# Matmuls that fill PE's waits before the dispatch, a joint dispatch of four tiles, and four small moves of other work

## The reference

```python
x = x + _L0_xattn_ref(_layernorm(x), ctx_1024, ctx_1024, ...)   # 16 heads, softmax over 1024 keys
x = x + _L0_attn_ref(_layernorm(x), ...)                        # S4 convolution over the 8 batches, then silu
x = x + _L0_ffn_ref(_layernorm(x), ...)                         # 16 experts, each token weighs its best 4
x = x + _L1_xattn_ref(_layernorm(x), ctx_1024, ctx_1024, mask, gamma, beta)
x = x + _L1_attn_ref(_layernorm(x), ...)                        # Mamba: conv, step size, recurrence h = At * h + Xt
x = x + _L1_ffn_ref(_layernorm(x), ...)                         # 8 experts top 2, and a shared one
```

## Time and profile before

| | us |
|---|---|
| median of 3 runs | 731.85 (731.85 to 731.97) |
| the profiled execution | 729.76 |
| its span, first to last instruction | 728.0 |
| granted TensorE clock, mean | 0.987 |

### The profile page before, as it was taken

The page is one execution under the profiler, slowest core; times in us unless marked ns, Lnnn a source line. Parts: engine busy times, 40 slices in busy tenths (PEclk is TensorE's granted clock), DMA queues, the critical chain, the costliest instruction groups (busy, mean ns, idle before and its releaser), DMA issues.

```text
span 728.0 us, 15573 instructions
## 1 busy us (share of the span) xinstructions
PE 683.5 (94%) x5722; PEld 558.3 (77%) x5722; DVE 539.4 (74%) x1205; ACT 412.5 (57%) x790; POOL 432.3 (59%) x455
## 2 busy tenths in 40 slices
PE   6799999999999978699999999999999899999997
PEld 3577777777787767599999999997457466666786
DVE  5788787877787886037777777763657899998676
ACT  3565756656655542266666666652336886665442
POOL 4658634646456226567788778745414698898130
PEclk9999999999999999799999999999999999999999
DMA  8301101101009392599989898995784610001000
GB/s 343 118 2 59 59 1 58 50 8 58 0 0 354 118 386 92 213 370 381 396 335 336 327 350 340 335 362 183 285 343 153 234 59 1 0 1 45 1 0 30
DMA packets 20477, 123.51 MB, mean 170 GB/s; under 512 B 2288, under 2 KB 6784, under 8 KB 13120
## 3 DMA queue, kind: packets, MB, share of 16 engines
q1 hardware_dynamic: 17488, 114.72, 41.4%
q0 software_dynamic: 2928, 8.00, 3.0%
HBM read 111.90 MB, written 10.81 MB: 169 GB/s over the span
## 4 chain that ended last, share of the span: by engine, by line
PE 77%; DVE 10%; ACT 5%; POOL 4%; issue 3%; DMA 1%; another core or an unknown queue 0%; DVEq 0%; SPq 0%; ACTq 0%; POOLq 0%; PEldq 0%
PE banks L2233 66%; PE banks L2301 8%; DVE shown L2094 2%; POOL inject L1016 2%; DVE banks L2101 1%; DVE negmax_raw L1618 1%; PE banks L2532 1%; ACT banks L1385 1%; PE banks L2848 1%; ACT probs L1097 1%; DMA table<-in_table 1%; DVE shown L2111 1%; ACT turned_back L1396 1%; PE banks L2688 0%
## 5 line engine op out<-in xcount | busy, mean ns | idle before, releaser
L2233 PE MATMUL banks<-xT,raw 128*128 128x128 f32 x992 | 151.6, 276 | 0.6 <-DVE xT L1882 0.6
L2233 PEld LDWEIGHTS banks<-xT,raw 128*128 128x128 f32 x992 | 135.5, 192 | 3.5 <-issue 1.1
L947 POOL TENSOR_TENSOR w_lo<-raw,w_hi 128x1024 fp32r<-128x1024 f32 x50 | 118.0, 2383 | 1.8 <-ACT w_hi L1217 1.0
L1248 ACT ACTIVATE banks<-banks,later 128x128 f32<-128x128 f32 x200 | 67.9, 339 | 56.3 <-PE banks L2233 54.9
L1888 DVE CAST mid_hi<-banks 128x128 fp32r<-128x128 f32 x200 | 57.8, 289 | 33.6 <-ACT banks L1248 31.8
L1127 ACT ACTIVATE probsT<-banks 128x512 f32<-128x512 f32 x68 | 40.1, 597 | 73.4 <-PE banks L2301 73.2
L1016 POOL TENSOR_TENSOR inject<-BCbc,drive 128x1024 f32<-128x1024 f32 x31 | 72.7, 2362 | 13.0 <-DVE shown L2094 7.7
L1097 ACT ACTIVATE probs<-banks,negmax 128x1024 f32<-128x1024 f32 x64 | 71.2, 1112 | 12.2 <-DVE negmax L1620 10.3
L1618 DVE TENSOR_REDUCE negmax_raw<-banks 128x1 f32<-128x1024 f32 x64 | 77.5, 1211 | 0.6 <-PE banks L2233 0.6
L2233 PE MATMUL banks<-w_hi,mid_hi 128*128 128x256 f32 x200 | 72.5, 362 | 0.0
L2301 PE MATMUL banks<-table,probs 128*128 128x128 f32 x512 | 69.6, 279 | 0.7 <-DVE probsT L1591 0.7
(11 more groups left out here) (358 smaller groups left out, 1763.7 us busy)
## 6 DMA issues: line engine op xcount, KB each, us to landing
raw<-in_w SPq DMA_DIRECT2D x31, 2048.0 KB, 8.9
ctx_raw<-in_ctxT SPq DMA_DIRECT2D x8, 1024.0 KB, 4.8
ctxT<-in_ctxT SPq DMA_DIRECT2D x4, 2048.0 KB, 9.3
ctxN<-in_ctxN SPq DMA_DIRECT2D x4, 2048.0 KB, 13.5
x_slots<-zero SPq DMA_DIRECT2D x1, 3968.0 KB, 12.5
y_slots<-y_tile POOLq DMA_DIRECT2D x29, 128.0 KB, 7.0
wf<-in_w SPq DMA_DIRECT2D x9, 384.0 KB, 5.3
BCbc<-bc_rows SPq DMA_DIRECT2D x6, 512.0 KB, 6.8
```

The lines of the kernel that those rows point to most:

```text
L947: nc.gpsimd.tensor_tensor(w2_lo[i % WB][:, cols], raw[i % WB][:, EW // 2:][:, cols], w2_hi[i % 2][:, cols].bitcast(F32), ALU.subtract).the ...
L1248: nc.scalar.activation(to, held, ACT.Gelu, bias=b1[:, bass.ds(at + u, 1)]).then_inc(gelu_done, 1)
L2233: return nc.tensor.matmul(o, lhsT, rhs, start=start, stop=stop)
```

## The change

1. `run_on` issues a float32 matmul of the identity with 128 or 256 columns of `later` into a bank that is free. Nine of them stand between and behind the routing's pieces (three of 128 columns), and three in `count_rows` (one of 128) (its bank is now called COUNT_BANK, still 3). No result uses them.
2. `largest` gets four more columns, filled once with the lowest value; `match_replace` reads columns 0 to 3 and 8 to 11. The four `memset`s are gone.
3. HOT is 5: `hot_rest` has four tiles, `dispatch_rest` multiplies 512 columns and stands at n = 4 (REST_AT). `x_rows` is read from tile 5 on; its place in memory stays (ROWS_FROM = 4). The spreads are turned at (3, 0) and (3, 4), four units later.
4. The mask terms are made in quarters behind the stores of tiles 6 to 13.
5. `step_end` becomes `step_size` and `step_drive`; for the step of chunks 2 and 3 the first stands one unit earlier. The skip term of chunks 0 to 2 stands behind `turn_states` of g = 7.
6. In the first batch ACT makes part 0 of the second batch's `ctx_hi` ahead of the second exponential.
7. The two late splits are made in halves, behind units 26, 27 and 29, 30.

```diff
-HOT = 4
+HOT, REST_AT = 5, 4
+ROWS_FROM = 4
-LAST = 2
+LAST, MASK_FROM = 2, 6
-SPREAD_AT = tuple(UNITS * i + u for i, u in ((2, 4), (3, 0)))
+SPREAD_AT = tuple(UNITS * i + u for i, u in ((3, 0), (3, 4)))
-SKIP_AT = (6, 6, 6, 4)
+LAST_SKIP = 4
...
-                if i < 2:
-                    mask_term(i)
+                if MASK_FROM <= i < MASK_FROM + 8:
+                    mask_term(*divmod(i - MASK_FROM, 4))
...
-                    if n - 1 in SPLIT1_AT:
-                        split_low1(SPLIT1_AT[n - 1])
-                    if g == GROUPS // 2 and m + 1 < CC:
-                        step_end(m + 1)
+                    for half in range(2):
+                        if n - 1 - half in SPLIT1_AT:
+                            split_low1_half(SPLIT1_AT[n - 1 - half], half)
+                    if m + 1 < CC:
+                        if g == GROUPS // 2 - (1 if m else 0):
+                            step_size(m + 1)
+                        if g == GROUPS // 2:
+                            step_drive(m + 1)
...
-                    if d == 0 and later_one:
-                        context_high(b + 1, 1 - par, range(1, DC))
+                    if d == 0:
+                        context_high(b + 1, 1 - par, range(1, DC) if later_one else range(1))
...
-                    if d == 0 and not later_one:
-                        context_high(b + 1, 1 - par)
+                        context_high(b + 1, 1 - par, range(1, DC))
...
-                    order.step(nc.vector.max(largest[:, t, :], logits[:, t, :]))
-                    order.step(nc.vector.memset(largest[:, t, TOP0:], LOWEST))
-                    order.mark(nc.vector.match_replace(left[:, t, :], largest[:, t, :], ranked[:, t, :], TAKEN))
+                    order.step(nc.vector.max(largest[:, t, 0:8], logits[:, t, :]))
+                    first_four = largest[:, t, :].rearrange("p (a b) -> p a b", b=TOP0)[:, 0::2, :]
+                    order.mark(nc.vector.match_replace(left[:, t, :], first_four, ranked[:, t, :], TAKEN))
...
+                run_on(SQUARE_BANK, 1, P)
                 pe.wait_ge(sel_ready, sel_before + 2)
...
+                run_on(SQUARE_BANK, 2)
+
+            def run_on(bank, times=1, columns=D):
+
+                for _ in range(times):
+                    mm(pb(bank)[:, 0:columns], ident, later[:, 0:columns], True, True)
...
             turn_tokens(3, 0, ROUTE_BANKS)
+            run_on(LOGIT_BANKS[2], 1, P)
             turn_tokens(3, 1, ROUTE_BANKS)
...
+            run_on(LOGIT_BANKS[2])
+            route(0)
+            run_on(LOGIT_BANKS[2])
+            turn_tokens(3, 2, ROUTE_BANKS)
+            run_on(LOGIT_BANKS[2], 1, P)
+            route(1)
+            turn_tokens(3, 3, ROUTE_BANKS)
+            run_on(COUNT_BANK, 1, P)
+            route(2)
+            run_on(COUNT_BANK)
+            route(3)
+            run_on(COUNT_BANK, 3)
...
-                if n == 1:
+                if n == REST_AT:
                     dispatch_rest()
...
-                if g == SKIP_AT[m]:
-                    pe.wait_ge(skip_made, 2 * GS + m + 1)
-                    mm(pb(Y_BANK), skip_diag[:, m * P:(m + 1) * P], aT[:, m, :], False, False)
+                if m == CC - 1 and g == LAST_SKIP:
+                    add_skip(m)
...
+                    if m < CC - 1 and g == GROUPS - 2:
+                        add_skip(m)
```

More of the change, by code:

```diff
@@ L331, in build @@
                 mask += [sb("phase", f"mask{q}", [P, KEYS], I32) for q in range(2, TC)]
-                assert mask_at >= aliased + (X_PIECES[2] - HOT) * D * 4 and place["phase"] <= aliased + (TILES - WB + 2 - HOT) * D * 4
+                assert mask_at >= aliased + (X_PIECES[2] - ROWS_FROM) * D * 4 and place["phase"] <= aliased + (TILES - WB + 2 - ROWS_FROM) * D * 4
             ctxN2.append(sb("phase" if p else "stage", f"ctxN2{p}", [P, 2, KC, D]))
@@ L1043, in split_low1, with split_low1_half @@
                 nc.gpsimd.tensor_tensor(f_lo[n][:], wf[n][:], f_hi[n][:].bitcast(F32), ALU.subtract).then_inc(f_lo_ready, 1)
+            def split_low1_half(n, half):
+                if half == 0:
+                    pool.wait_ge(f_hi_ready, n + 1)
+                cols = slice(half * FW // 2, (half + 1) * FW // 2)
+                done = nc.gpsimd.tensor_tensor(f_lo[n][:, cols], wf[n][:, cols], f_hi[n][:, cols].bitcast(F32), ALU.subtract)
+                if half:
+                    done.then_inc(f_lo_ready, 1)
             def split_whole1(n):
@@ L1733, in _ @@
             order.mark(nc.vector.memset(ranked[:, :, E0:], LOWEST))
+            order.mark(nc.vector.memset(largest[:, :, 8:], LOWEST))
             order.mark(nc.vector.memset(restart[:, :, 0:1], 0.0))
@@ L2597, in _ @@
             turn_tokens(3, 0, ROUTE_BANKS)
+            run_on(LOGIT_BANKS[2], 1, P)
             turn_tokens(3, 1, ROUTE_BANKS)
-            for t in range(TC):
-                route(t)
-                if t + 2 < TC:
-                    turn_tokens(3, t + 2, ROUTE_BANKS)
+            run_on(LOGIT_BANKS[2])
[10 more added lines that the diff above has]
+            run_on(COUNT_BANK, 3)
             def turn_spread(k):
```

37 lines of the change are left out of this document (22 added, 15 removed).

## The result

| us | before | with the change |
|---|---|---|
| median, this comparison (4 runs each) | 731.89 (731.85 to 731.97) | 727.05 (726.15 to 727.38) |
| the profiled execution | 729.76 | 726.15 |
| its span | 728.0 | 724.4 |
| mean granted clock in it | 0.987 | 0.993 |

The ratio is 0.9934, with a 95% interval of 0.9923 to 0.9946: faster by 4.8 us (4.0 to 5.6). Two later comparisons gave 0.9942 and 0.9943. By the two profiled executions alone the gain is 3.6 us, 1.2 less than by the medians. So two questions stand: which of my terms were wrong within the profile, and what do the medians hold that the profile does not.

What follows compares the result with a forecast made beforehand. PE, at 94% busy, was taken as the bound. Terms -1.25 - 0.4 - 0.2 + 0.95 - 1.47 = -2.4 took 729.76 to 727.4; plus the 2.1 median offset: 729.4, range 727.4 to 732.4.

Steps and rivals of the forecast that it cites:

- Context: First batch: ctx_hi made earlier on ACT ends PE's 1.93 us wait for ctx_lo; -1.25 us, from -1.93 to 0.
- Routing: Routing and first dispatch: four memsets leave DVE's chain, so the scatters come earlier; -0.4 us, from -0.6 to 0.
- The cover of the scatters: First tiles: PE's standstill until the scatters land hides dispatch gains and costs; only the scatters' -0.4 us counts.
- the stand: First tiles, about 288 to 300: PE nearly still, read as late word of finished matmuls while scatters run.
- Joint dispatch, turning and the new wait: Expert tiles: larger dispatch 0 (bound +0.85), tile 4's turning dropped -0.2, PE's wait at n = 24 +0.95 us.
- Recurrence: Scans: moving the skip term and step size shortens DVE's waits for ACT and inject; -1.47 us, from -0.8 to -1.6.
- Masks, late halves: Mask quarters hidden in POOL's idle time, 0; last chunk's DVE wait of 0.99 goes but PE is late, 0, bound -0.1.
- rival on the clock behind the scatters: Same as Rival A: full clock at once when PE goes on after the scatters, saving 1.6 us; chance 0.14.
- Rival A: Behind the stand: clock full at once instead of half over 3.2 us of PE's work, saving 1.6: 727.8; chance 0.14.
- B: First batch and recurrence: PE as the bound takes back half of -1.25 - 1.47, giving 730.8; chance 0.23.
- C: First tiles: the joint dispatch falls into the stand, delaying tile 1's xT; +1.7 to +3.3 us, about 734; chance 0.13.
- D: Routing: extra matmuls don't hold the clock, dispatch stays at 3.41 us; 729.4 to 729.8, chance counted within the forecast's 0.50.

Runs made afterwards that it cites:

- run with the stand filled: 14 unused float32 matmuls ahead of the downs of units 9 to 11, against the changed kernel with tile 4's rows copied first: median 729.21 us.

## Why the prediction was wrong

The sign was right, and most mechanisms; the size was not. The measured 727.05 lies 2.35 us under the forecast. Of these 1.2 are the step from the profile to the median, which fell from 2.1 to 0.9 us; 0.6 are a start of the first exponential that happened to be early, which is luck of one execution; and 0.6 are errors of the terms that partly cancel.

- **Context.** Predicted -1.25. `k_hi` came 1.22 earlier against the first exponential, as worked out, and 0.9 to 1.0 of it was left by the ninth. A little too high for an execution whose clock doesn't fall there.
- **Routing.** Predicted -0.4 by way of the scatters. The first scatter started 0.5 earlier against the convolution, but took 1.75 us, and the second stood where it did: 39.5 us to the last scatter in both kernels. The term was 0. It hid two parts: without the memsets but also without the extra matmuls it was 38.62 us in one profile, with the extra matmuls but with the memsets 39.92.
- **The cover of the scatters.** Right for the dispatch in one execution: from the last scatter to the 28th `y_tile` little changed (185.35 and 185.15 in the mean). But the stage is no constant: over all profiles of all variants it took 184.6 to 187.8 us. I also wrote that the 16 scatters are issued in 288 to 300; nine of them were issued before 288. And my reading of the stand was wrong or at least incomplete: I took it for late word of finished matmuls, and matmuls that wait for no word are slow there too.
- **Joint dispatch, turning and the new wait.** Predicted 0, -0.2 and +0.95; the wait measured 1.00, and all three together gave 1.0003, an interval that holds my +0.75 as well. The ledger has no such loss though the wait lies in it, so something of about 0.75 stood against the wait, which I had not; what, is not shown. In the first profile the changed kernel's PE had one unit more behind it when the scatters had landed.
- **Recurrence.** Predicted -1.47, measured -1.88 in every profile. DVE's 0.53 did not fall to 0.14 but to nothing, twice, and the first border gave 0.41, not 0.33.
- **Masks, late halves.** Predicted 0 and 0, and no worth showed.

In the stages of the profile that makes -1.0, 0, 0, -1.9 and -0.1, or -3.0 against my -2.4, which would still have been within the range (728.9).

**The step that failed** is the one that looked like bookkeeping: "the median of the runs is 2.1 above the profiled execution, so **729.4** as a median". I carried these 2.1 us over as a constant. For the changed kernel it was 0.9, 0.6 and 0.9 us in three comparisons, for the kernel before 2.1 and 2.6. With 0.9 the same terms give 728.3. The offset went down as the mean clock went up: the changed kernel has 0.991 to 0.995 in 15 executions, the kernel before 0.977 to 0.988. One place that makes the difference is shown: behind the wait for `ctx_lo` half clock of 3.4 us cost 1.5 to 1.6 us in three of the seven profiles that have this wait unfilled (one of the three of the unchanged kernel), and stood in none of the twelve with the context move. The second is only argued: in 265 to 282 half clock lasts 6.8, 10.2 or 13.7 us without the extra matmuls and is gone in all twelve profiles with them, but 10.2 cost nothing over 6.8, and the loss beside the 13.7 came without it too. No profile caught an execution of the kernel before above 730.5 us, and filling the wait at 32 raised neither the clock nor the speed of the median.

So the two clock terms were mis-sized, and by how much depends on the run: the context move, predicted 1.25, is worth 2.2 us alone and 0.9 to 1.5 when undone; the extra matmuls, predicted 0 beyond the scatters' 0.4, 1.1 alone (0.2 to 2.0) and 0 to 0.7 when undone. With the recurrence's 1.9 the parts make 5.2, or 4.5 with the 2.6 that the first two gave together, and 4.2 to 4.8 was measured; the intervals of about 1 us on each part leave that agreement loose.

The Trainium skill says that the window by which the clock is granted is free-running (TensorE: Matmul & The Clock Gate, Part 1), and shows its effect at the start of a kernel. The trace agrees in that executions of the kernel before, with an identical wait of 1.93 us, had the clock fall behind it or not; no run here shows that the window is the cause. I used the rule for a rival on the clock behind the scatters, where it fell in all twenty profiles, and not at the short wait, where it fell in some.

Rival A's 727.8 was the nearest price to the measured time, and by luck: the full clock behind the stand that it is made of did not come, half clock lay on 2.95 us of PE's work there. B, C and D did not occur. Of D, the extra matmuls not holding the clock, I said that it costs 0 to 0.4; the runs leave 0 to 2.

Open stay: in how many executions of before each of the two stretches appears, since only a profile shows the place; why filling the wait at 32 gained nothing in the median; what sets how far PE is when the scatters have landed, which moved the next stage by up to 2.6 us between profiles; and what slows PE's instructions while the scatters run.

## What to carry to other kernels

One profile is one draw. Where a short idle time of PE ends next to busy work, price it twice: the wait, and half clock behind it in some share of the executions (here 0.9 to 1.0 us, and 1.5 more in three of seven profiles); and before adding an offset between the profile and the median, look at the mean clock of the timed runs, because a change that removes idle time may remove the offset too. Matmuls without use gave 1.1 us in the routing, nothing in the wait at 32, and cost 2.5 us where PE's own instructions come slowly: see first that idle time ahead of them isn't the sequencer's ("issue").

## What was unexpected of the hardware

- While POOL's 16 indirect scatters were landing, PE took up one instruction in 0.70 us, though it waited for nothing that the profile shows, from about 292 to 298 us (run with the stand filled).
- The first scatter's issue took 1.75 us where it began 0.04 us behind DVE's first write of `hot_rest`, 1.23 us where it began 0.18 us ahead of it, and the last ones took 0.96. That DVE is the cause was not tested.
- The same program had half clock at one place or not from execution to execution, and in the routing it had it in all three profiles, for 6.8 or 10.2 us.
